# A state-space scan kernel in which each partition of a token tile holds four consecutive tokens instead of every 128th

## What is computed

```python
x = x + s6(layernorm(x), A_log, D, x_proj_w, dt_proj_w, dt_proj_b)
x = x + int8_linear(layernorm(x), weight_q, weight_scale, bias)

# s6: xp = x @ x_proj_w.T -> d_rank (64), B (16), C (16)
#     delta = softplus(d_rank @ dt_proj_w.T + dt_proj_b)
#     for each state n of 16, along the 2048 tokens:
#         h = exp(-exp(A_log[:, n]) * delta) * h + delta * B[:, n] * x
#         y += h * C[:, n]
#     y = y + x * D
# int8_linear: each token's row is scaled by its largest magnitude / 127, rounded,
#     multiplied by weight_q (512 x 512), and scaled back; then bias is added
```

## Time and profile before

| | |
|---|---|
| time, median of 3 runs | 2826.95 us (2826.89 to 2827.49) |
| the profiled execution, first to last instruction | 2824.8 us |
| what lies around it, against the median | 2.15 us |
| mean granted clock of TensorE | 0.998 of 2.4 GHz |
| chunks | 32; one period in the middle takes 86.5 us |
| busy: PE, DVE, ACT, POOL | 98%, 96%, 97%, 98% |
| DMA traffic | 319.11 MB in 197312 packets |

### The profile page before, as it was taken

How to read it: one execution, slowest core, us unless ns; L and a number is a source line. 1 busy time by engine, 2 the same in 40 slices (tenths; PEclk the granted TensorE clock), 3 DMA queues, 4 the chain that set the end, 5 groups by cost and what they waited for, 6 DMA issues and landing times.

```text
span 2824.8 us, 59754 instructions
## 1 busy us (share of the span) xinstructions
PE 2778.3 (98%) x22624; PEld 2515.1 (89%) x22624; DVE 2721.6 (96%) x2801; ACT 2729.4 (97%) x5084; POOL 2762.4 (98%) x1137
## 2 busy tenths in 40 slices
PE   7999999999999999999999999999999999999998
PEld 6899899898998898998989989989989899899897
DVE  6999999999999999999999999999999999999997
ACT  7999999999999999999999999999999999999995
POOL 4999999999999999999999999999999999999998
PEclk9999999999999999999999999999999999999999
DMA  5334544444444345444444444453544544445432
GB/s 189 91 98 95 136 114 116 124 102 107 118 123 115 100 102 132 112 121 121 94 118 116 125 112 104 102 132 110 123 113 93 128 116 118 116 106 119 100 95 63
DMA packets 197312, 319.11 MB, mean 113 GB/s; under 512 B 93025, under 2 KB 93025, under 8 KB 180642
## 3 DMA queue, kind: packets, MB, share of 16 engines
q1 hardware_dynamic: 164290, 250.29, 29.1%
q0 software_dynamic: 32736, 65.02, 15.1%
HBM read 212.70 MB, written 102.56 MB: 112 GB/s over the span
## 4 chain that ended last, share of the span: by engine, by line
POOL 61%; issue 32%; PE 4%; DMA 1%; DVE 0%; ACT 0%; SPq 0%; POOLq 0%; DVEq 0%
POOL A L532 47%; POOL C L549 5%; POOL C L541 3%; POOL XN L484 2%; POOL out L556 1%; POOL out L564 1%; PE Y L777 1%; POOL PW L501 1%; PE PB L755 1%; PE PB L752 1%; PE Y L773 0%; SPq L402 0%; DVE A L913 0%; PE PM L817 0%; POOL RO L503 0%
## 5 line engine op out<-in xcount | busy, mean ns | idle before, releaser
L532 POOL TENSOR_TENSOR A<-A,CB 128x2048 f32<-128x2048 f32 x511 | 2348.9, 4721 | 40.1 <-DMA CB<-c_rows 27.5
L913 DVE TENSOR_TENSOR_SCAN A<-A,CAR,PB 128x512 f32<-128x512 f32 x1536 | 1844.7, 1259 | 23.6 <-PE PB L752 13.1
L595 ACT ACTIVATE A<-DEL,an 128x512 f32<-128x512 f32 x2048 | 1376.3, 719 | 0.4
L777 PE MATMUL Y<-idf,A 128*128 128x128 f32 x8192 | 1125.8, 273 | 2.2 <-POOL A L532 1.8
L777 PEld LDWEIGHTS Y<-idf,A 128*128 128x128 f32 x8192 | 945.7, 141 | 83.1 <-issue 67.2
L616 ACT ACTIVATE DB<-XN,BC 128x512 f32<-128x512 f32 x1472 | 1003.1, 719 | 1.1 <-PE PB L755 1.1
L755 PE MATMUL PB<-idf,DB 128*128 128x128 f32 x5888 | 857.9, 274 | 24.3 <-DVE A L913 18.6
L755 PEld LDWEIGHTS PB<-idf,DB 128*128 128x128 f32 x5888 | 683.7, 142 | 55.1 <-DVE A L913 37.2
L913 DVE TENSOR_TENSOR_SCAN A<-A,PB 128x512 f32<-128x512 f32 x512 | 591.1, 1203 | 28.0 <-PE PB L752 13.4
L752 PEld LDWEIGHTS PB<-DG,XN 128*128 128x128 f32 x4608 | 565.6, 192 | 42.4 <-issue 32.4
L752 PE MATMUL PB<-DG,XN 128*128 128x128 f32 x4608 | 600.0, 275 | 2.4 <-DVE A L913 2.4
(11 more groups left out here) (96 smaller groups left out, 1652.2 us busy)
## 6 DMA issues: line engine op xcount, KB each, us to landing
CB<-c_rows SPq DMA_DIRECT2D x128, 1024.0 KB, 5.9
DG<-b_diag SPq DMA_DIRECT2D x160, 256.0 KB, 5.8
X<-in_x SPq DMA_DIRECT2D x31, 1024.0 KB, 5.7
out<-bib SPq DMA_DIRECT2D x31, 1024.0 KB, 8.6
out<-X POOLq DMA_DIRECT2D x31, 1024.0 KB, 9.4
out<-C POOLq DMA_DIRECT2D x31, 1024.0 KB, 9.0
b_diag<-DG SPq DMA_DIRECT2D x2, 1280.0 KB, 11.0
b_diag<-BC SPq DMA_DIRECT2D x160, 2.0 KB, 5.7
```

The lines of the kernel that those rows point to most:

```text
L532: gp.tensor_tensor(A[s % NA][:, :, :], A[s % NA][:, :, :], CB[:, s % (4 * NG), :].unsqueeze(1).broadcast_to([128, KB, L]), ALU.mult).then_ ...
L595: act.activation(A[s % NA][:, g, :], DEL[k % 2][:, g, :], ACT.Exp, scale=an[:, g, n:n + 1])\
L777: i = pe.matmul(Y[j][:, g * 128:(g + 1) * 128], A[s % NA][:, g, j * 128:(j + 1) * 128], idf[:, :], is_transpose=True, start=False, stop=(n ...
L913: dve.tensor_tensor_scan(A[s % NA][:, g, :], A[s % NA][:, g, :], PB[(4 * s + g) % NPB][:, :], init, ALU.mult, ALU.add).then_inc(s_scan, 1)
```

## The change

A partition now holds tokens 4p to 4p + 3 of the chunk, in slots 0 to 3. So a partition's four rows are 8 KB in one piece in memory, in the load of x, in the write of the bias and in both adding DMAs; in the four single loads of the first chunk and the four stores of the last, rows stay single (2 KB) and lie 8 KB apart. Slot j now stands for every fourth column of the time layout, beginning at j. The transposes that go from rows to time write every fourth column of their PSUM bank (L752, L755, L807), and those from time to rows read every fourth column of A, XT, XP and DEL as the stationary operand (L777, L773, L824, L845). Nothing else changes: no instruction is added or removed, and no wait.

```diff
 SP
-xf[p * L:(p + 1) * L, :].rearrange("(t p) d -> p t d", p=128)           # load
+xf[p * L:(p + 1) * L, :].rearrange("(p t) d -> p t d", t=T)
-of[p * L:(p + 1) * L, :].rearrange("(t p) d -> p t d", p=128)           # put_bias
+of[p * L:(p + 1) * L, :].rearrange("(p t) d -> p t d", t=T)
-sp.dma_start(X[0][:, j, :], xf[j * 128:(j + 1) * 128, :])
+sp.dma_start(X[0][:, j, :], xf[0:L, :].rearrange("(p t) d -> p t d", t=T)[:, j, :])
-sp.dma_start(of[p * L + j * 128:p * L + (j + 1) * 128, :], rows(p)[:, j, :])
+sp.dma_start(of[p * L:(p + 1) * L, :].rearrange("(p t) d -> p t d", t=T)[:, j, :], rows(p)[:, j, :])
 POOL
-gp.dma_start(of[p * L:(p + 1) * L, :].rearrange("(t p) d -> p t d", p=128), X[p % NX][:, :, :],   # add_x
+gp.dma_start(of[p * L:(p + 1) * L, :].rearrange("(p t) d -> p t d", t=T), X[p % NX][:, :, :],
-gp.dma_start(of[p * L:(p + 1) * L, :].rearrange("(t p) d -> p t d", p=128), C[:, :, :],           # add_c
+gp.dma_start(of[p * L:(p + 1) * L, :].rearrange("(p t) d -> p t d", t=T), C[:, :, :],
 PE
-pe.matmul(PB[u % NPB][:, j * 128:(j + 1) * 128], XN[...], DG[...], ...)                           # tb
+pe.matmul(PB[u % NPB][:, j:L:T], XN[...], DG[...], ...)
-pe.transpose(PB[u % NPB][:, j * 128:(j + 1) * 128], DB[...], idf[:, :])
+pe.transpose(PB[u % NPB][:, j:L:T], DB[...], idf[:, :])
-pe.matmul(Y[j][...], XT[:, g, j * 128:(j + 1) * 128], dd[:, g, :], ...)                           # th
+pe.matmul(Y[j][...], XT[:, g, j:L:T], dd[:, g, :], ...)
-pe.matmul(Y[j][...], A[s % NA][:, g, j * 128:(j + 1) * 128], idf[:, :], is_transpose=True, ...)
+pe.matmul(Y[j][...], A[s % NA][:, g, j:L:T], idf[:, :], is_transpose=True, ...)
-pe.transpose(bank(p, g)[:, j * 128:(j + 1) * 128], XN[...], idf[:, :])                            # x_t
+pe.transpose(bank(p, g)[:, j:L:T], XN[...], idf[:, :])
-pe.transpose(PM[:, j * 128:j * 128 + 96], XP[0:96, j * 128:(j + 1) * 128], idf[0:96, 0:96])       # b_c
+pe.transpose(PM[:, j * 128:j * 128 + 96], XP[0:96, j:L:T], idf[0:96, 0:96])
-pe.transpose(bank(p, j)[:, g * 128:(g + 1) * 128], DEL[p % 2][:, g, j * 128:(j + 1) * 128], ...)  # dl_t
+pe.transpose(bank(p, j)[:, g * 128:(g + 1) * 128], DEL[p % 2][:, g, j:L:T], ...)
```

More of the change, by code:

```diff
@@ L369, in load @@
                     sp.wait_ge(s_c, T * (p - NX + 1))
-                sp.dma_start(X[i][:, :, :], xf[p * L:(p + 1) * L, :].rearrange("(t p) d -> p t d", p=128))\
+                sp.dma_start(X[i][:, :, :], xf[p * L:(p + 1) * L, :].rearrange("(p t) d -> p t d", t=T))\
                   .then_inc(s_xl[i], 16)
@@ L418, in put_bias @@
                     sp.wait_ge(s_w2, 64)
-                sp.dma_start(of[p * L:(p + 1) * L, :].rearrange("(t p) d -> p t d", p=128),
+                sp.dma_start(of[p * L:(p + 1) * L, :].rearrange("(p t) d -> p t d", t=T),
                              bib[:, :].unsqueeze(1).broadcast_to([128, T, D])).then_inc(s_bi[p % 2], 16)
             for j in range(T):
-                sp.dma_start(X[0][:, j, :], xf[j * 128:(j + 1) * 128, :]).then_inc(s_x0[j], 16)
+                sp.dma_start(X[0][:, j, :], xf[0:L, :].rearrange("(p t) d -> p t d", t=T)[:, j, :]).then_inc(s_x0[j], 16)
             sp.dma_start(wxs[:, :, :], wxp.rearrange("(k p) e -> p k e", p=128)).then_inc(s_w, 16)
@@ L444, in put_last @@
                     sp.wait_ge(s_fp if j < 2 else s_fv, j % 2 + 1)
-                    sp.dma_start(of[p * L + j * 128:p * L + (j + 1) * 128, :], rows(p)[:, j, :]).then_inc(s_end, 16)
+                    sp.dma_start(of[p * L:(p + 1) * L, :].rearrange("(p t) d -> p t d", t=T)[:, j, :], rows(p)[:, j, :]).then_inc(s_end, 16)
             run(put_last=put_last, load=lambda p, i: later(p), store_c=lambda p, i: store_c(p), load_c=load_c,
@@ L751, in tb @@
                     if j < ROWS.get(n, 0):
-                        i = pe.matmul(PB[u % NPB][:, j * 128:(j + 1) * 128], XN[k % 2][:, j, g * 128:(g + 1) * 128],
+                        i = pe.matmul(PB[u % NPB][:, j:L:T], XN[k % 2][:, j, g * 128:(g + 1) * 128],
                                       DG[:, (NDG * k + DIAG.index(n)) % NR, j, :], start=True, stop=True)
                     else:
-                        i = pe.transpose(PB[u % NPB][:, j * 128:(j + 1) * 128],
+                        i = pe.transpose(PB[u % NPB][:, j:L:T],
                                          DB[(scaled(s) - 1) % ND][:, j, g * 128:(g + 1) * 128], idf[:, :])
@@ L772, in th @@
                     for g in range(KB):
-                        i = pe.matmul(Y[j][:, g * 128:(g + 1) * 128], XT[:, g, j * 128:(j + 1) * 128], dd[:, g, :],
+                        i = pe.matmul(Y[j][:, g * 128:(g + 1) * 128], XT[:, g, j:L:T], dd[:, g, :],
                                       start=(g == 0), stop=False, skip_group_check=True)
@@ L776, in th @@
                 for g in range(KB):
-                    i = pe.matmul(Y[j][:, g * 128:(g + 1) * 128], A[s % NA][:, g, j * 128:(j + 1) * 128], idf[:, :],
+                    i = pe.matmul(Y[j][:, g * 128:(g + 1) * 128], A[s % NA][:, g, j:L:T], idf[:, :],
                                   is_transpose=True, start=False, stop=(n == NS - 1), skip_group_check=True)
@@ L806, in x_t @@
                 for j in range(T):
-                    i = pe.transpose(bank(p, g)[:, j * 128:(j + 1) * 128], XN[p % 2][:, j, g * 128:(g + 1) * 128],
+                    i = pe.transpose(bank(p, g)[:, j:L:T], XN[p % 2][:, j, g * 128:(g + 1) * 128],
                                      idf[:, :])
@@ L823, in b_c @@
                 for j in range(T):
-                    i = pe.transpose(PM[:, j * 128:j * 128 + 96], XP[0:96, j * 128:(j + 1) * 128], idf[0:96, 0:96])
+                    i = pe.transpose(PM[:, j * 128:j * 128 + 96], XP[0:96, j:L:T], idf[0:96, 0:96])
                 i.then_inc(s_bct, 1)
@@ L844, in dl_t @@
                 for g in range(KB):
-                    i = pe.transpose(bank(p, j)[:, g * 128:(g + 1) * 128], DEL[p % 2][:, g, j * 128:(j + 1) * 128],
+                    i = pe.transpose(bank(p, j)[:, g * 128:(g + 1) * 128], DEL[p % 2][:, g, j:L:T],
                                      idf[:, :])
```

## The result

The changed kernel takes **3025.96 us** (4 runs, 3024.34 to 3027.46) against 2827.22 us of the kernel before beside it (2826.89 to 2828.58): ratio 1.070, 95% interval 1.0687 to 1.0717. It is 199 us slower, where 11 us less were forecast, and lies above the range. No instruction was added, so the time must have gone into instructions that got longer, or into waits.

The account below looks back on a forecast made before the run. Four engines were taken as balanced, POOL leading the chain with PE close behind. From 2824.8 us, plus 2.15, less 11 for POOL's DMAs and 0 for the rest: about 2816 us; own range 2803 to 2821, 8 in 10 2800 to 2920.

Parts of the forecast that it names:

- The bound: Whole kernel: four engines balanced at 96% to 98% busy; PE has 0.6 to 0.8 us to spare a period, some 20 us.
- SP's DMAs, worth 0: Load of x, bias write and last stores on SP: as many DMAs, no mid-run waits for them, so 0.
- POOL's two DMAs, 11 us: Adding DMAs on POOL: cheaper issue saves 0.5 us a period, 0.35 us comes through over 31 periods, 11 us less.
- the sign: POOL after the adding DMA L556: distance to the next L532 falls from 1.18 to 0.9 us if issue gets cheaper.
- Strided writes, 0: PE's 344 PSUM writes a chunk with a 16-byte step: float32 uses half the write rate seen, so 0 ns.
- Strided weight loads, 0: PE's 308 weight loads a chunk with a 16-byte step: stay within 109 ns, so 0, with less ground than the writes.
- The second: Rival on PE's strided operands: a step halves the float32 rate; 3880 us (loads), 4010 (writes), about 5080 (both); chance 0.20.
- the third: Rival on L777, L755 and L752: some ns more per strided instruction, PE hiding 0.96 ns each; chance 0.17.
- its example: Surcharge of 2.5 ns on each strided PE instruction, as L752 has over L777 before the change: 2859 us.
- Its second example: Surcharge four times as large as 2.5 ns on each strided PE instruction: 2994 us.

Follow-up runs that it names:

- the version with five and two buffers: Changed kernel, but POOL writes products slot by slot into two buffers of their own, five A instead of seven, XT kept slot by slot: 3074.84 us.

## Why the prediction was wrong

*The bound.* Right that PE would be the next to bind once POOL got cheaper, and that any cost on PE would show almost in full. Its spare time was taken too small: 7.2 us a period were added and 6.2 came out, so **1.0 us** was hidden where 0.6 to 0.8 had been worked out; over the run 7.2 x 32 - 199 = 31 us, not 20. A PE that never stops takes 92.63 - 7.2 = 85.4 us for the old work, so the sum of 85.7 us was 0.3 too high. This moved nothing of weight.

*SP's DMAs, worth 0.* Right: no wait for a DMA in the middle of the run. The load of x lands in 5.0 us instead of 5.7; the bias write takes 8.6 us as before.

*POOL's two DMAs, 11 us.* Right in the sum, and shown alone: 12.6 us with the DMAs changed by themselves. The terms were off both ways: by the records POOL saved 1.0 us a period, twice the 0.5 taken, and of that 0.36 us came through, a third where some 70% had been allowed. That the product is so near is in part luck. Nor did the sign come that was named for it: behind L556 POOL now waits for ACT's carries, so the distance to the next L532 is 1.42 us and not 0.9. The saving is real and buys nothing in the changed kernel, where PE is the bound.

*Strided writes, 0.* Right, for the reason given: the bf16 rows showed twice the rate that float32 uses, and a step halves it (56 to 109 ns in bf16, 109 to 109 in float32 transposes).

*Strided weight loads, 0.* **This step failed.** The prediction carried the argument of the write port over to the load, "because they too pass one 4-byte word in 0.85 ns". But the row under it showed how fast PE starts instructions, not how fast a load can go. For writes there was a row with twice the rate; for float32 loads there was none, and the missing row should have kept the chance of a penalty high. The runs showed that such a load can set the distance itself: L773's passes went from 112 to 232 ns and L777's transposes from 109 to 121.5 ns, 7.2 us a period with L824 and L845, where the prediction had 0. For float32 passes at the 2.4 GHz level the distance is 1.8 ns for each 16-byte line, hidden up to 112 ns. Why the same loads cost a transpose only 12 ns, and bf16 next to nothing, the runs do not settle.

*The rivals.* The second (a halved rate, 219 ns) was right for L773 (232 ns) and wrong for L777, for which it gave 109 ns more; the third (a surcharge of some ns) was right for L777, at 12 ns, five times its example, and wrong for L755 and L752, which had none. Its second example is also summed wrongly: four times 2.5 ns on 652 x 32 instructions is 209 us, less 20, or 3016 us, not 2994. That this is near the measured time is chance, since the price lay on other instructions. Neither foresaw that passes and transposes would differ. With both prices as measured, 7.2 us in each of 32 periods, and the forecast's own 20 us to spare, the sum would have been 210 us more, 11 above the measured 199: a time between "surcharge", worked out up to 2994 us, and "halved", from 3880 us, that the prediction did not have as a case; its range had ended at 2920 us.

The rule of lines of 16 bytes (the Trainium skill, SBUF — State Buffer, in the part on the DMA port swizzle) agrees with the float32 passes, 118, 173 and 233 ns at 64, 96 and 128 lines, and not with the transposes, where two words of each line cost 120 ns as one does. The same place takes a step of four float32 values, or eight bf16 values, as free: for bf16 that is nearly so (61 ns for 56), for a float32 pass it is not (233 ns for 112), and the measurement decides. The rule that a write into PSUM that is not contiguous slows matmuls (the Trainium skill, PSUM — Partial Sum Buffer, Specifications (TRN2)) agrees for bf16 and not for float32.

## What to carry to other kernels

Ask of a step on each PE operand apart: in float32, writes into PSUM may step for nothing, while the stationary and the moving operand want neighbours, or at least a step of 2, in matmuls of two passes most of all, and a transpose pays for a step of 2 in its stationary operand as much as for 4. An argument that an operand has room to spare needs a row that shows it going faster; the pace at which instructions start is only a lower bound on what it can do. Longer rows for DMAs issued by POOL do pay (1.0 us a pair here, by the records, from 512 to 128 runs, of which 0.36 us a period came through), but only as long as POOL is the bound.

## What the runs showed of the hardware

- A float32 pass whose 128 weights lie 4, 8, 12, 16 or 32 bytes apart starts every 112, 118, 173, 233 or 238 ns; a float32 transpose every 109, 120, 115, 120 or 113 ns. That step 8 is cheaper than step 4 for transposes was not expected and is not explained.
- At step 4 a pass takes 233 ns at either level of PE's clock (granted 1.00 with 128 columns streamed, 0.50 with 32); at steps 2 and 3 it takes 118 and 173 ns at the upper level and 213 ns at the lower.
- bf16 loads of 128 columns cost nothing extra at steps 2 and 4 (56 ns) and 5 ns at step 8 (61 ns).
- A float32 pass that streams its moving operand starts every 114 ns at step 2 and every 227 ns at step 4.
- A strided write halves the rate in bf16 (56 to 109 ns) and costs float32 nothing.
- POOL's product takes the same time when it writes with a step of 512 bytes (4613 ns on average in the version with five and two buffers, 4632 ns in the run with the DMAs alone).
- ACT's copy of 96 x 512 float32 into XP with a step of 16 bytes takes 1108 ns in place of 574; with a step of 8 bytes, 635 ns.
- POOL's record of issuing an adding DMA of 1 MB is, for C, 1291 to 1312 ns at 512 runs, 1218 ns at 256 and 833 to 884 ns at 128. For X it differs from kernel to kernel at the same number of runs, which is not explained: 1294 or 1716 ns at 512 runs, 1581 ns at 256, 876 to 1099 ns at 128.
